# A decoder layer with experts on Trainium2: one block to the end, the feed-forward part reordered, bias and residual on TensorE

## The chip, the core and the metric

The program runs on one NeuronCore of one Trainium2 chip. The metric is the device time in microseconds (us). The engines are TensorE (PE in the profile, its weight loads PEld), VectorE (DVE), ScalarE (ACT), GpSimd (POOL) and SyncE (SP, which here only issues DMAs). Each engine works through a queue of its own in program order; engines wait for one another at semaphores. TensorE's clock has two levels, 1.2 and 2.4 GHz; the profile gives the granted clock as a share of full speed.

## The reference

16 sequences of 128 tokens and 128 features pass through a convolution mixer, a self-attention and a cross-attention of 16 heads, a feed-forward layer of 512 and, last, a small layer per token: the first 16 tokens of a sequence have an expert each, the other 112 share one. After every part stands a norm. Cut to what follows the attentions:

```python
h = gelu(x @ fc1_w + fc1_b)
x = layernorm(x + h @ fc2_w + fc2_b, ln3_g, ln3_b)
...
x = _layernorm(x + xattn)                       # x4 in the kernel
xe = x[:, :16];  y = _layernorm(xe, g_e, b_e)
out_e = gelu(einsum('bnd,ndh->bnh', y, W1_e) + b1_e) @ W2_e + b2_e      # an expert per token
xr = x[:, 16:];  out_s = gelu(_layernorm(xr, g_s, b_s) @ W1_s + b1_s) @ W2_s + b2_s
out = _layernorm(x + concatenate([out_e, out_s], axis=1))
```

## The kernel before

Every engine's queue is written out by hand in Python, as calls of small helpers. `mixer_and_attentions` is one block: the mixer works on pairs of sequences, the attentions on 32 items (16 sequences, twice), in a software pipeline over `p`. In a step TensorE runs the projections of item p + 1, the transposes of item p - 1 (`transposes`, four quarters), the output projection of item p - 2 (`out_proj`, L485), scores and `p_v` (L469). After the loop (L593 to L602) it does the first feed-forward layer (`hidden`, L236) of groups 0 and 1, mixed with the last items, and the second layer (`fc2_sum`, L253) of group 0. A group is four sequences, a chunk 128 of the 512 hidden features; `hidden` multiplies a chunk in three fp32r passes (a product of high and low parts) into banks 0 to 3. ScalarE applies the gelu (`gelu_hidden`, L244) from the bank to `hT`, of which there are two.

`feed_forward` (L1163) is a second block: no engine enters it before all have left the first. For each of the four groups VectorE computes `residual3` (the sum and its moments), `gained` and `outer_sums` (ln3 and the sum of the outer residual, with its moments), `outer_shift`, `experts_inputs`, `output_sum`, `output_statistics`, `output_shift`. The powers to -0.5 are POOL's (`inverse_ln3`, `inverse_outer` for the inner and the outer norm in one instruction, `inverse_out`), and POOL adds the second bias to X4 (`second_bias`, L1550, 128x512). ScalarE applies the norms (`z_normal`, `outer_normal`, `z_affine`, `output`) and the gelus. TensorE transposes (`z_transposes`, L1247), runs the shared first layer (`shared_w1`, L1256), the shared second layer (`shared_w2`, L1261) and, at the end, the 16 experts: `experts_w1` (L1269) needs the transposed tokens of all groups, `experts_w2` their gelu; VectorE's `experts_sums` adds the tokens' own rows (`xE`), which went through DRAM, and `experts_output` normalises. The queue of VectorE in that block (L1491 to L1525) sets the order in which groups overlap. SP loads both expert weights at the start of the block (L1219), parks X4's expert rows, reads them back, and stores four groups and four quarters of experts.

## Time and profile before

| | us |
|---|---|
| median of 3 runs | 522.64 (522.31 to 524.3) |
| the profiled execution's own time | 525.09 |
| its span, first to last instruction | 522.5 |
| TensorE busy | 473.1 |
| VectorE busy | 387.5 |
| ScalarE busy | 367.9 |
| POOL busy | 257.0 |
| mean granted clock of TensorE | 0.968 |

The span is the part of an execution between its first and its last instruction. Busy times of engines overlap, so they don't add up to it. A row of a timeline has the start, the duration, the engine, the line, the operation, the tile written and the tiles read, the shapes, how many alike were merged, and in brackets how long the engine was idle before it and what ended that.

### The profile page before, as it was taken

To read this page: it belongs to the slowest core of one execution; us is meant where nothing else is said; L and a number is where in the kernel's file an instruction comes from. 1 tells how busy PE (TensorE), PEld (TensorE's weight loads), DVE (VectorE), ACT (ScalarE), POOL (GpSimd) and SP (SyncE) were. 2 spreads that over 40 slices of the span, in tenths; PEclk is the share of its full clock that TensorE was granted. 3 is DMA by queue.
4 is the path that set the end of the run, shared out by engine and by line. 5 is a ranking of instruction groups with operands and counts; after the bars stand their busy time and mean duration, and the time that the engine had idled before them with its cause. 6 is when DMAs were issued, how large, how long until landed. Compare 5 with 4: busy or idle time off the path is not lost. (4 is left out here: it accounts for less than half of the span.)

```text
span 522.5 us, 14070 instructions
## 1 busy us (share of the span) xinstructions
PE 473.1 (91%) x4624; PEld 435.1 (83%) x4624; DVE 387.5 (74%) x1848; ACT 367.9 (70%) x1393; POOL 257.0 (49%) x343
## 2 busy tenths in 40 slices
PE   4789889999998989999999999999999998987573
PEld 4678779989998989999999999999999977876462
DVE  4667678888888887877887788778778776379832
ACT  3547877868686878887777777777778767537551
POOL 1443356666566565554445454455544455344530
PEclk9899899999999999999999999999999999999955
DMA  8830000000000004000000000000000000040003
GB/s 241 261 138 2 0 4 1 2 2 2 1 3 1 2 2 120 3 2 1 3 1 3 3 2 2 2 1 3 1 3 3 2 2 2 0 162 4 6 13 80
DMA packets 15719, 14.17 MB, mean 27 GB/s; under 512 B 2848, under 2 KB 13344, under 8 KB 15520
## 3 DMA queue, kind: packets, MB, share of 16 engines
q1 hardware_dynamic: 14240, 12.88, 7.9%
q8 instruction: 37, 0.61, 0.5%
q10 hardware_dynamic: 1408, 0.40, 0.4%
q14 instruction: 34, 0.28, 0.2%
HBM read 12.10 MB, written 1.18 MB: 25 GB/s over the span
## 5 line engine op out<-in xcount | busy, mean ns | idle before, releaser
L611 ACT ACTIVATE P<-P,at_negmax 128x128 f32<-128x128 f32 x512 | 198.9, 396 | 83.3 <-DVE at_negmax L788 83.3
L1038 POOL TENSOR_TENSOR P<-P,at_inv 128x512 f32<-128x512 f32 x128 | 136.4, 1076 | 129.9 <-DVE at_inv L798 129.8
L814 DVE COPY at_PT<-late_bank 128x512 f32<-128x512 f32 x128 | 87.7, 688 | 36.7 <-PE late_bank L448 36.5
L788 DVE CUSTOM_DVE_ANT_0 P<-late_bank,maskb 128x128 f32<-128x128 f32 x512 | 111.3, 286 | 1.5 <-PE late_bank L465 1.5
L611 ACT ACTIVATION_READ_ACCUMULATOR P<-P,at_negmax 128x1 f32 x512 | 100.1, 195 | 0.0
L448 PE MATMUL late_bank<-ident,P 128*128 128x128 f32 x512 | 77.0, 274 | 4.6 <-DVE at_negmax L788 2.8
L448 PEld LDWEIGHTS late_bank<-ident,P 128*128 128x128 f32 x512 | 59.9, 141 | 11.1 <-issue 6.4
L465 PE MATMUL late_bank<-at_k,at_q 64*128 64x128 f32 x1024 | 65.8, 278 | 0.9 <-DVE at_k L806 0.9
L465 PEld LDWEIGHTS late_bank<-at_k,at_q 64*128 64x128 f32 x1024 | 59.7, 188 | 4.8 <-issue 1.2
L480 PE MATMUL late_bank<-at_PT,V 128*64 128x128 f32 x1024 | 63.0, 276 | 0.0
L480 PEld LDWEIGHTS late_bank<-at_PT,V 128*64 128x64 f32 x1024 | 55.2, 137 | 3.9
L806 DVE COPY at_k<-late_bank 128x512 f32<-128x512 f32 x64 | 44.2, 691 | 12.6 <-PE late_bank L75 11.4
L788 DVE DVE_READ_ACCUMULATOR2_ANT at_negmax<- 128x1 f32 x512 | 42.5, 83 | 0.0
L621 ACT ACTIVATE at_q<-late_bank 128x512 f32<-128x512 f32 x64 | 37.6, 587 | 4.1 <-PE late_bank L75 4.1
L1056 POOL TENSOR_TENSOR at_N<-at_N,row_ln_g 128x128 f32<-128x128 f32 x32 | 14.7, 460 | 48.8 <-DVE at_N L839 48.8
L630 ACT ACTIVATE V<-late_bank 128x512 f32<-128x512 f32 x64 | 37.5, 586 | 0.0
L496 PE MATMUL late_bank<-wo_sa,at_OT 128*128 128x128 f32 x256 | 31.6, 276 | 3.6 <-DVE x1T_lo L936 3.6
L638 ACT ACTIVATE at_OT<-late_bank 128x512 f32<-128x512 f32 x64 | 34.1, 586 | 0.0
L496 PEld LDWEIGHTS late_bank<-wo_sa,at_OT 128*128 128x128 f32 x256 | 29.8, 192 | 4.6 <-issue 4.6
L522 PE MATMUL late_bank<-xT_hi,w_hi 128*128 128x256 f32 x72 | 23.2, 323 | 9.9 <-DVE xT_lo L857 7.0
L496 PE MATMUL late_bank<-wo_ca,at_OT 128*128 128x128 f32 x256 | 31.2, 275 | 0.0
L496 PEld LDWEIGHTS late_bank<-wo_ca,at_OT 128*128 128x128 f32 x256 | 29.9, 192 | 0.1
(177 smaller groups left out, 1062.3 us busy)
## 6 DMA issues: line engine op xcount, KB each, us to landing
ctxT_raw<-in_ctxT SPq DMA_DIRECT2D x1, 1024.0 KB, 9.3
out<-xres SPq DMA_DIRECT2D x4, 224.0 KB, 2.9
x<-in_xT SPq DMA_DIRECT2D x1, 768.0 KB, 9.7
xres<-in_x SPq DMA_DIRECT2D x1, 768.0 KB, 13.1
tap_rows<-in_short_wT SPq DMA_DIRECT2D x3, 192.0 KB, 4.4
sa_wq_raw<-in_sa_wq SPq DMA_DIRECT2D x1, 512.0 KB, 7.7
sa_wk_raw<-in_sa_wk SPq DMA_DIRECT2D x1, 512.0 KB, 8.8
sa_wv_raw<-in_sa_wv SPq DMA_DIRECT2D x1, 512.0 KB, 9.8
```

What stands on the lines that cost most here:

```text
L448: last = nc.tensor.transpose(banks[T_BANK[g % 2]][:, h * 128:(h + 1) * 128], P[:, n % 2, HQ * g + h, :], k.ident[:])
L465: last = nc.tensor.matmul(score_bank(h), q[rows, t % 2, h // 2, pair], kk[rows, t % 2, h // 2, pair], start=True, stop=True)
L480: last = nc.tensor.matmul(banks[O_BANK[h // 8]][part:part + 64, h // 2 % 4 * 128:(h // 2 % 4 + 1) * 128], V[:, n % 2, h * DH:(h + 1) * DH] ...
L496: last = nc.tensor.matmul(banks[W_BANK][:, 0:128], OT[:, n % 2, c, :], out_w[att(n)][:, c, :], start=(c == 0), stop=(c == H // 2 - 1))
L611: last = nc.scalar.activation(P[:, n % 2, h, :], P[:, n % 2, h, :], ACT.Exp, scale=-1.0, bias=negmax[:, n % 2, h:h + 1], accum_out=total[: ...
L621: nc.scalar.activation(q[:, t % 2, u:u + 2, :], banks[UNIT_BANK[0]][:].rearrange("p (h l) -> p h l", h=2), ACT.Copy, scale=NEG_SCALE).then ...
L630: nc.scalar.activation(V[:, n % 2, half * 512:(half + 1) * 512], banks[V_BANK][:], ACT.Copy).then_inc(v_ok, 1)
L638: nc.scalar.activation(OT[:, n % 2, 4 * o:4 * o + 4, :], banks[O_BANK[o]][:].rearrange("p (c l) -> p c l", c=4), ACT.Copy).then_inc(ot_ok, 1)
L788: last = nc.vector.tensor_tensor_reduce(P[:, n % 2, h, :], score_bank(h), k.maskb[:, cols(n)], scale=1.0, scalar=3.0e38, op0=ALU.add, op1= ...
L806: nc.vector.tensor_copy(kk[:, t % 2, u - 1:u + 1, :], banks[UNIT_BANK[1]][:].rearrange("p (h l) -> p h l", h=2)).then_inc(k_ok, 1)
L814: nc.vector.tensor_copy(PT[:, HQ * g:HQ * g + HQ, :], banks[T_BANK[g % 2]][:].rearrange("p (h l) -> p h l", h=HQ)).then_inc(pt_ok, 1)
L1038: nc.gpsimd.tensor_tensor(tile, tile, inv[:, n % 2, HQ * g:HQ * g + HQ].unsqueeze(2).to_broadcast([128, HQ, 128]), ALU.mult).then_inc(norm ...
```

## The change

The body of `feed_forward` moves into the block of `mixer_and_attentions`; there is one block. Its tiles lie where queries and keys and where the weights of self-attention lay. Step p = 32 of the loop is written out and mixed with first-layer chunks. `hidden` uses banks 0 and 1 in turn, `hT` has three parts, and two first-layer chunks of the next group stand ahead of each second layer. The inner and outer powers on POOL become two instructions of 4 columns. POOL's `second_bias` goes; TensorE adds the bias (in high and low parts, times an identity) into the bank of the shared second layer before it, one bank per group, and for groups 2 and 3 also X4 (`add_x4`), so that their statistics and norms read the bank (`SUMMED = 2`). The experts' bias is added alike (`experts_second_bias`). Half of group 3's inner norm (`z_normal_rest`) and all of group 3's last norm (`last_output`) are VectorE's. The shared gelu covers all 128 tokens. Constants for the bias are made at p = 18 on ScalarE (`bias_high`) and VectorE (`bias_low`). The order of all queues in the feed-forward part is new; ScalarE issues two of the experts' four stores.

Three places follow, by the order of instructions. TensorE at the handover, before: item 31's last transposes, the output projection of item 30, `p_v` of item 31, the first chunk.

```order
L448 MATMUL late_bank3<-ident,P 128x128 x4
L496 MATMUL late_bank7<-wo_ca,at_OT 128x128 x8
L480 MATMUL late_bank4<-at_PT,V 64x128 x8
L480 MATMUL late_bank5<-at_PT,V 64x128 x8
L505 MATMUL late_bank7<-ident,at_X 128x128
L73 MATMUL late_bank0<-x1T_hi,fc1_hi 128x512
```

The same place now, from the second quarter of the transposes on.

```order
L534 MATMUL late_bank3<-ident,P 128x128 x4
L72 MATMUL late_bank0<-x1T_hi,fc1_hi 128x512
L73 MATMUL late_bank0<-x1T_lo,fc1_hi 128x512
L74 MATMUL late_bank0<-x1T_hi,fc1_lo 128x512
L72 MATMUL late_bank1<-x1T_hi,fc1_hi 128x512
L73 MATMUL late_bank1<-x1T_lo,fc1_hi 128x512
L74 MATMUL late_bank1<-x1T_hi,fc1_lo 128x512
L669 MATMUL late_bank6<-bias2_hi,ident_r 128x512
L669 MATMUL late_bank6<-bias2_lo,ident_r 128x512
L534 MATMUL late_bank2<-ident,P 128x128 x4
L534 MATMUL late_bank3<-ident,P 128x128 x4
L582 MATMUL late_bank7<-wo_ca,at_OT 128x128 x8
```

Two chunks of group 0 and the bias of group 0 moved between the second and the third quarter.

VectorE from group 3's residual to its outer sums, before (`ffR` is the residual, `xres` the output sum of group 1).

```order
L1395 TENSOR_TENSOR ffR<-late_bank4,xres 128x512
L1384 BN_STATS ffstats<-ffR 128x6 x4
L1388 BN_AGGR ffmv<-ffstats 128x2 x4
L1399 TENSOR_SCALAR ffvar<-ffmv 128x4
L1449 TENSOR_TENSOR xres<-late_bank7,x1 128x512
L1384 BN_STATS ffstats<-xres 128x6 x4
L1388 BN_AGGR ffmv<-ffstats 128x2 x4
L1455 TENSOR_SCALAR ffvar<-ffmv 128x4
L1407 SCALAR_TENSOR_TENSOR N3<-ffR,ffmv,ln3_g 128x128 x4
L1418 SCALAR_TENSOR_TENSOR N3<-N3,ffrstd,x1 128x128 x4
L1384 BN_STATS ffstats<-N3 128x6 x4
```

The same place now.

```order
L1262 TENSOR_TENSOR ffR<-late_bank4,xres 128x512
L1299 SCALAR_TENSOR_TENSOR ffshift<-ffmv,ffrstd 128x4
L1250 BN_STATS ffstats<-ffR 128x6 x4
L1254 BN_AGGR ffmv<-ffstats 128x2 x4
L1268 TENSOR_SCALAR ffvar<-ffmv 128x4
L1304 SCALAR_TENSOR_TENSOR ffshift<-ffmv,ffrstd 128x4
L1276 SCALAR_TENSOR_TENSOR N3<-ffR,ffmv,ln3_g 128x128 x4
L1323 TENSOR_TENSOR zE<-late_bank5,gainT 128x64
L1327 TENSOR_TENSOR zE<-zE,shiftT 128x64
L1287 SCALAR_TENSOR_TENSOR N3<-N3,ffrstd,x1 128x128 x4
L1250 BN_STATS ffstats<-N3 128x6 x4
```

The output sum and statistics of group 1 are gone from here (those of group 0 from group 2's place alike), and the shifts of group 2 came in.

TensorE's last rows, before: transposes of group 3, shared first layer, experts around the shared second layer.

```order
L1252 MATMUL late_bank5<-ident,N5 128x128 x4
L1259 MATMUL late_bank6<-zT,w1s 128x512
L1274 MATMUL late_bank0<-zE,w1e 128x16 x3
L1265 MATMUL late_bank7<-w2,gT 128x128 x4
L1274 MATMUL late_bank0<-zE,w1e 128x16 x13
L1283 MATMUL late_bank1<-w2e,hE 32x128 x16
```

TensorE's last rows now.

```order
L669 MATMUL late_bank0<-bias2_hi,ident_r 128x512
L669 MATMUL late_bank0<-bias2_lo,ident_r 128x512
L697 MATMUL late_bank4<-bias2_hi,select 128x128 x4
L697 MATMUL late_bank4<-bias2_lo,select 128x128 x4
L674 MATMUL late_bank3<-x1,ident 128x512
L648 MATMUL late_bank5<-ident,N5 128x128 x4
L679 MATMUL late_bank3<-w2,gT 128x128 x4
L689 MATMUL late_bank1<-zE,w1e 128x16 x16
L657 MATMUL late_bank7<-zT,w1s 128x512
L707 MATMUL late_bank4<-w2e,hE 32x128 x16
L674 MATMUL late_bank0<-x1,ident 128x512
L679 MATMUL late_bank0<-w2,gT 128x128 x4
```

The experts' first layer stands ahead of group 3's shared first layer, and group 3's shared second layer is the last matmul of all; five rows of bias and X4 stand ahead of the transposes.

The diff, cut to its core (the helpers that only moved are left out):

```diff
+    k.overlay(ctx, allocate_self_weights, allocate_last)
...
-    k.hT = (k.V[:].rearrange("p b (c l) -> p (b c l)", l=128).rearrange("p (c b l) -> p c b l", b=GRP, l=128),
-            k.P[:, 0].rearrange("p (c b) l -> p c b l", b=GRP))
+    k.hT = tuple(k.P[:, i].rearrange("p (c b) l -> p c b l", b=GRP) for i in range(2)) + (
+        k.V[:].rearrange("p b (c l) -> p (b c l)", l=128).rearrange("p (c b l) -> p c b l", b=GRP, l=128),)
...
-def hidden(k, pe, g, blocks=range(FF // 128)):
-
-    for c in blocks:
-        wait(pe, k.h_ok, 4 * g + c - 3)
-        mm_split(k.nc, k.late_banks[c][:], k.fc1, np.s_[:, c * 128:(c + 1) * 128], k.x1T,
+def hidden(k, pe, g, chunks=range(FF // 128)):
+
+    for c in chunks:
+        wait(pe, k.h_ok, 4 * g + c - 1)
+        mm_split(k.nc, k.late_banks[c % 2][:], k.fc1, np.s_[:, c * 128:(c + 1) * 128], k.x1T,
                  np.s_[:, g * GCOLS:(g + 1) * GCOLS]).then_inc(k.fc1_mm, 1)
 
 
-def gelu_hidden(k, act, g):
-    for c in range(FF // 128):
+def gelu_hidden(k, act, g, chunks=range(FF // 128)):
+    for c in chunks:
         act.wait_ge(k.fc1_mm, 4 * g + c + 1)
         if c == 0:
-            wait(act, k.fc2_mm, g - 1)
-        k.nc.scalar.activation(k.hT[g % 2][:, c], k.late_banks[c][:].rearrange("p (b l) -> p b l", b=GRP), ACT.Gelu,
+            wait(act, k.fc2_mm, g - 2)
+        k.nc.scalar.activation(k.hT[g % 3][:, c], k.late_banks[c % 2][:].rearrange("p (b l) -> p b l", b=GRP), ACT.Gelu,
                                bias=k.fc1_b[:, c:c + 1]).then_inc(k.h_ok, 1)
...
+            sp.wait_ge(s_mm, 2 * ITEMS)
...
+            sp.wait_ge(ne_ok, 1)
+            for i in (0, 1):
+                store_experts(sp, i)
+            store_group(sp, LAST)
...
+            def second_bias(g):
+
+                if g == 0:
+                    pe.wait_ge(k.bias_lo, 1)
+                    pe.wait_ge(v_ok, 2 * ITEMS)
+                elif g < LAST:
+                    pe.wait_ge(pt_ok, 4 * ITEMS)
+                else:
+                    pe.wait_ge(k.h_ok, 4 * NGRP - 1)
+                for part in (k.bias2.hi, k.bias2.lo):
+                    nc.tensor.matmul(quarter(W2_BANK[g]), k.ident_r[:], part[:].unsqueeze(1).to_broadcast([128, GRP, 128]),
+                                     start=(part is k.bias2.hi), stop=False)
+
+            def add_x4(g):
+                pe.wait_ge(x4_ok, g + 1)
+                nc.tensor.matmul(banks[W2_BANK[g]][:], k.ident[:], X4[:, group(g)], start=False, stop=False)
...
+            def experts_second_bias():
+                pe.wait_ge(r3_ok, NGRP)
+                for part in (k.bias2.hi, k.bias2.lo):
+                    for c in range(NEXP // EQ):
+                        nc.tensor.matmul(banks[E2_BANK][:, c * 128:(c + 1) * 128],
+                                         k.select[0:NEXP, c].rearrange("e i s -> e (i s)"), part[0:NEXP, :],
+                                         start=(part is k.bias2.hi and c == 0), stop=False)
...
+            x_transpose(ITEMS - 4)
+            transposes(ITEMS - 1, 0)
+            transposes(ITEMS - 1, 1)
+            pe.wait_ge(k.ff_lo, 1)
+            pe.wait_ge(max_ok, 4 * ITEMS)
+            wait_result(0)
+            hidden(k, pe, 0, (0, 1))
+            second_bias(0)
+            transposes(ITEMS - 1, 2)
+            transposes(ITEMS - 1, 3)
+            out_proj(ITEMS - 2)
+            p_v(ITEMS - 1)
             x_transpose(ITEMS - 3)
-            pe.wait_ge(k.ff_lo, 1)
-            pe.wait_ge(pt_ok, 4 * ITEMS)
-            hidden(k, pe, 0)
+            hidden(k, pe, 0, (2, 3))
             out_proj(ITEMS - 1)
+            wait_result(1)
+            hidden(k, pe, 1, (0, 1))
             x_transpose(ITEMS - 2)
-            hidden(k, pe, 1)
+            fc2_sum(k, pe, 0)
             x_transpose(ITEMS - 1)
-            pe.wait_ge(ot_ok, 2 * ITEMS)
-            fc2_sum(k, pe, 0)
+            hidden(k, pe, 1, (2, 3))
+            wait_result(2)
+            hidden(k, pe, 2, (0, 1))
+            next_fc2(1)
+            hidden(k, pe, 2, (2, 3))
+            wait_result(3)
+            hidden(k, pe, 3, (0, 1))
+            next_fc2(2)
+            z_transposes(0)
+            hidden(k, pe, 3, (2, 3))
+            shared_w1(0)
+            next_fc2(3)
+            z_transposes(1)
+            second_bias(1)
+            shared_w2(0)
+            shared_w1(1)
+            z_transposes(2)
+            second_bias(2)
+            shared_w2(1)
+            shared_w1(2)
+            second_bias(3)
+            experts_second_bias()
+            add_x4(2)
+            z_transposes(3)
+            shared_w2(2)
+            experts_w1()
+            shared_w1(3)
+            experts_w2()
+            add_x4(3)
+            shared_w2(3)
...
+            gelu_hidden(k, act, 0, (0, 1))
             ot_out(ITEMS - 1, 0)
             ot_out(ITEMS - 1, 1)
-            gelu_hidden(k, act, 0)
+            xT_high(ITEMS - 3)
+            gelu_hidden(k, act, 0, (2, 3))
+            gelu_hidden(k, act, 1, (0, 1))
             xT_high(ITEMS - 2)
-            gelu_hidden(k, act, 1)
             xT_high(ITEMS - 1)
+            gelu_hidden(k, act, 1, (2, 3))
+            gelu_hidden(k, act, 2)
+            z_normal(0)
+            gelu_hidden(k, act, 3, (0, 1))
+            outer_normal(0)
+            z_affine(0)
+            gelu_hidden(k, act, 3, (2, 3))
+            z_normal(1)
+            gelu_shared(0)
+            outer_normal(1)
+            z_affine(1)
+            z_normal(2)
+            gelu_shared(1)
+            z_affine(2)
+            outer_normal(2)
+            gelu_shared(2)
+            z_normal(3)
+            outer_normal(3)
+            z_affine(3)
+            output_normal(0)
+            gelu_experts()
+            gelu_shared(3)
+            output_normal(1)
+            output_normal(2)
...
+            def bias_high():
+                nc.scalar.activation(k.ident_r[:], k.ident[:], ACT.Copy).then_inc(k.bias_hi, 1)
...
+            def z_normal_rest():
+
+                vec.wait_ge(zT_mm, LAST - 1)
+                for b in range(GRP // 2, GRP):
+                    s = LAST * GRP + b
+                    last = nc.vector.tensor_scalar(N5[:, LAST % 2, b], N3[:, LAST % 2, b], mv3[:, 1, s, 0:1],
+                                                   rstd3[:, INNER_NORM, s:s + 1], ALU.subtract, ALU.mult)
+                last.then_inc(z_half_ok, 1)
...
+            def last_output():
+                vec.wait_ge(rstd_out, NGRP)
+                for b in range(GRP):
+                    s = LAST * GRP + b
+                    last = nc.vector.tensor_scalar(res[:, s], banks[W2_BANK[LAST]][:, b * 128:(b + 1) * 128],
+                                                   mv3[:, 2, s, 0:1], rstd3[:, OUT, s:s + 1], ALU.subtract, ALU.mult)
+                last.then_inc(last_ok, 1)
...
+            residual_sum(0)
+            residual_moments(0)
             xT_low(ITEMS - 1)
+            gained(0)
+            outer_sums(0)
+            inner_shift(0)
+            residual_sum(1)
+            residual_moments(1)
+            outer_shift(0)
+            gained(1)
+            outer_sums(1)
+            inner_shift(1)
+            residual_sum(2)
+            residual_moments(2)
+            outer_shift(1)
+            experts_inputs(0)
+            gained(2)
+            outer_sums(2)
+            residual_sum(3)
+            inner_shift(2)
+            residual_moments(3)
+            outer_shift(2)
+            gained(3)
+            experts_inputs(1)
+            outer_sums(3)
+            output_sum(0)
+            inner_shift(3)
+            z_normal_rest()
+            output_statistics(0)
+            outer_shift(3)
+            experts_inputs(2)
+            experts_inputs(3)
+            output_sum(1)
+            output_shift(0)
+            output_statistics(1)
+            experts_bias()
+            output_shift(1)
+            output_statistics(2)
+            experts_sums()
+            output_shift(2)
+            output_statistics(3)
+            experts_output()
+            last_output()
...
+            def inverse_outer(g):
+                pool.wait_ge(var_inner, g + 1)
+                nc.gpsimd.tensor_tensor(rstd3[:, INNER_NORM, group(g)], var3[:, INNER_NORM, group(g)],
+                                        k.half_neg[:, 0:GRP], ALU.pow).then_inc(rstd_inner, 1)
+                pool.wait_ge(var_outer, g + 1)
+                nc.gpsimd.tensor_tensor(rstd3[:, OUTER, group(g)], var3[:, OUTER, group(g)],
+                                        k.half_neg[:, 0:GRP], ALU.pow).then_inc(rstd_outer, 1)
...
-            def second_bias(g):
-                pool.wait_ge(x4_ok, g + 1)
-                nc.gpsimd.tensor_tensor(X4[:, seqs(g)], X4[:, seqs(g)],
-                                        k.bias2[:].unsqueeze(1).to_broadcast([128, GRP, 128]),
-                                        ALU.add).then_inc(x4b, 1)
...
```

## Rows read from the trace of the kernel before

**Rows 1.** The page: busy us, share of the span and instructions per engine.

```profile
PE 473.1 (91%) x4624; PEld 435.1 (83%) x4624; DVE 387.5 (74%) x1848; ACT 367.9 (70%) x1393; POOL 257.0 (49%) x343
```

**Rows 2.** Windows: stretch, length, busy us (instructions) of each engine, clock, DMA, GB/s.

```profile
15.00:20.00 5.00, 2.81 (x16) 2.60 (x15) 2.93 (x5) 2.53 (x6) 0.84 (x1) 0.79 0.44 128
...
286.00:298.00 12.00, 12.00 (x130) 11.26 (x130) 9.41 (x48) 9.36 (x41) 5.98 (x9) 1.00 0.00 1
475.00:480.00 5.00, 4.22 (x24) 3.42 (x23) 4.41 (x25) 3.74 (x8) 2.10 (x3) 1.00 0.01 2
...
490.00:495.00 5.00, 1.85 (x10) 0.97 (x8) 4.83 (x21) 3.12 (x8) 2.46 (x2) 1.00 0.04 8
495.00:500.00 5.00, 0.79 (x4) 0.72 (x4) 3.04 (x21) 3.18 (x8) 2.64 (x2) 0.58 0.00 0
```

**Rows 3.** Timeline of VectorE at step p = 16.

```profile
262.72 0.84 DVE L851 TENSOR_TENSOR fc_lo<-fc_raw,fc_hi 128x512 fp32r<-128x512 f32 x1 [0.83 <-ACT fc_hi L652]
```

**Rows 4.** Timeline of TensorE at the handover.

```profile
443.58 1.22 PE L448 MATMUL late_bank<-ident,P 128*128 128x128 f32 x8 [1.02 <-issue]
...
448.50 0.48 PE L73 MATMUL late_bank<-x1T_hi,fc_hi 128*128 128x512 f32 x1
...
451.33 1.95 PE L496 MATMUL late_bank<-wo_ca,at_OT 128*128 128x128 f32 x16
453.75 0.30 PE L505 MATMUL late_bank<-ident,at_X 128*128 128x128 f32 x1 [0.47 <-DVE at_R L826]
...
456.74 3.73 PE L258 MATMUL late_bank<-fc,V 128*128 128x128 f32 x32
```

**Rows 5.** Timeline of VectorE in the feed-forward part.

```profile
460.81 0.69 DVE L1395 TENSOR_TENSOR ffR<-late_bank,xres 128x512 f32<-128x512 f32 x1 [2.79 <-PEq L272]
...
477.24 0.69 DVE L1449 TENSOR_TENSOR xres<-late_bank,x 128x512 f32<-128x512 f32 x1 [0.38 <-PE late_bank L1265]
...
479.38 1.14 DVE L1407 SCALAR_TENSOR_TENSOR N<-ffR,ffmv,ln_g 128x128 f32<-128x128 f32 x4
...
483.45 1.06 DVE L1443 TENSOR_TENSOR zE<-zE,shiftT 128x64 f32<-128x64 f32 x1
...
486.07 0.23 DVE L1431 SCALAR_TENSOR_TENSOR ffshift<-ffmv,ffrstd 128x4 f32<-128x4 f32 x2 [1.46 <-POOL ffrstd L1541]
...
490.56 2.15 DVE L1407 SCALAR_TENSOR_TENSOR N<-ffR,ffmv,ln_g 128x128 f32<-128x128 f32 x4
...
495.32 0.16 DVE L1425 TENSOR_SCALAR ffvar<-ffmv 128x4 f32<-128x4 f32 x1
```

**Rows 6.** Timeline of POOL: a power of 4 columns.

```profile
463.10 1.05 POOL L1535 TENSOR_TENSOR ffrstd<-ffvar,half_neg 128x4 f32<-128x4 f32 x1 [0.46 <-DVE ffvar L1399]
```

**Rows 7.** Timeline of TensorE towards the end.

```profile
486.09 1.06 PE L1265 MATMUL late_bank<-w,gT 128*128 128x128 f32 x8
...
499.21 1.12 PE L1252 MATMUL late_bank<-ident,N 128*128 128x128 f32 x4 [6.43 <-ACT N L1315]
...
504.20 2.05 PE L1265 MATMUL late_bank<-w,gT 128*128 128x128 f32 x8
506.05 5.57 PE L1274 MATMUL late_bank<-zE,w1e 128*128 128x16 f32 x26
512.67 1.94 PE L1283 MATMUL late_bank<-w2e,hE 128*32 128x128 f32 x32 [1.06 <-ACT hE L1351]
```

**Rows 8.** Timeline of VectorE: its last operation.

```profile
518.01 1.11 DVE L1487 TENSOR_SCALAR rE<-rE,mv_e,rstd_e 128x128 f32<-128x128 f32 x4 [1.12 <-POOL rstd_e L1573]
```

**Rows 9.** DMA issues (count, size, us to landing), and SP's timeline of one.

```profile
out<-xres SPq DMA_DIRECT2D x4, 224.0 KB, 2.9
...
xE<-experts_out SPq DMA_DIRECT2D x4, 32.0 KB, 2.2
...
505.63 2.58 SPq L1229 DMA_DIRECT2D xE<-experts_out  x4
```

**Rows 10.** Timeline of TensorE in the mixer.

```profile
17.53 0.39 PE L522 MATMUL late_bank<-xT_hi,w_hi 128*128 128x256 f32 x1 [2.19 <-ACT C L668]
```

658 lines of the change are left out of this document (301 added, 357 removed).

## Prediction, made before the changed kernel ran

> **What bounds the kernel now.** I read the page first, then busy time by stage, then the timeline of one engine after another from 440 us, because the change leaves the program as it was up to there. TensorE is busy 473.1 of 522.5 us [rows 1], and in the middle of the second attention it is busy 12.00 of every 12.00 us while VectorE works 9.41 and ScalarE 9.36 [rows 2]: up to about 440 us TensorE alone sets the time. After 460 us this turns. From 490 to 495 us VectorE works 4.83 of 5 us and TensorE 1.85 [rows 2], so the feed-forward part is a chain on VectorE. After 495 us no engine is full: group 3 passes alone through transposes, experts, sums and norm, with TensorE at clock 0.50. I take three stretches: handover (441.35 to 460.81), VectorE's stretch (460.81 to 495.48, the end of the last variance of group 3), and the end (495.48 to 522.5).
>
> **What the sum is made against.** The profiled span is 522.5 us. That execution's own time was 525.09, the median of the timed runs 522.64. I predict the median, 0.1 above the span.
>
> **Before 440 us: nothing.** New there are the bias's high part and two constants (three small ScalarE copies) and its low part on VectorE at p = 18. The same kind of pair stands at p = 16 already, larger: VectorE waits 0.83 us and works 0.84 [rows 3], and TensorE shows no idle time behind it. Its cover is VectorE's 2.6 us of slack per 12 us; without it the price would be about 1 us. The expert weights' DMAs move up to the last scores (about 431 us), behind SP's loads, where nobody waits for SP. POOL's two clearings (0.5 us each) stand in front of the norm of item 30, whose input comes 3 us later.
>
> **Handover.** In the queue of before TensorE waits 1.02 us for the last transposes and 0.47 for item 30's result, then runs all eight first-layer chunks of groups 0 and 1 before the second layer of group 0 (3.73 us from 456.74) [rows 4]. A chunk takes (451.33 - 448.50) / 4 = 0.71 us [rows 4]. Now two chunks go into the 1.02 us gap, and two chunks of group 1 stand behind the second layer: -1.42 for those two and -1.49 for the gaps. Added are 0.46 for the two bias matmuls (each 512 columns in one pass, like a third of a chunk), 0.7 for new waits (a chunk needs item 28's low part, which lands 0.5 us after the transposes, and 0.2 at the output projection). The last x transpose (0.1) goes behind, and the end of the block costs 0.34 us from 460.47 to VectorE's start at 460.81 [rows 4, 5], of which an ordinary semaphore would take 0.07: -0.4 in all. Sum -2.1: the first residual starts at 458.7. Banks 0 and 1 alone now serve the first layer, so TensorE waits for each gelu (0.69 us against 0.71): 0.3 us twice, with VectorE's chain 0.7 us or more behind TensorE at every group.
>
> **VectorE's stretch.** It lasts 34.7 us. Removed ahead of group 3's sums are the output sum and statistics of groups 0 and 1, 2.14 us each (477.24 to 479.38) [rows 5]: -4.3. Removed are POOL's adds of the second bias: under them a 0.22 us operation took 1.06, four that take 1.13 took 2.15 [rows 5], a third 0.87 in place of 0.17: 0.84 + 1.02 + 0.70 = -2.6. The waits of 0.20, 0.18, 0.21, 0.38 and 1.46 us (the last for a POOL power of 8 columns behind such an add [rows 5]) go: -2.4. New: each inner shift stands directly behind its variance and waits for a power of 4 columns, 1.05 us [rows 6] and the two semaphores: 1.2 us for groups 0 and 1, 0.5 for group 2, where the next residual stands between: +2.9. One more low part, and split shifts: +0.4. Sum -6.0: 28.7 us, to 487.4. TensorE's second layers would end 0.7, 1.5 and 1.7 us before VectorE wants them, so TensorE does not set this stretch.
>
> **A rule against a row.** A power on POOL ran from 463.10 for 1.05 us [rows 6] while VectorE multiplied with two inputs from SBUF at its usual 1.13 us, so only the 128x512 adds block. The Trainium skill, SBUF — State Buffer, section "Who interferes with whom", says that any GpSimd instruction that reads SBUF excludes a VectorE one with two SBUF inputs. By the rule VectorE's half of the last inner norm could lose up to 0.8 us under group 3's second power; by the row it loses nothing, and that is what I take.
>
> **The end.** From 487.4: output sum 0.7, shift when the power has landed (488.5), half of the inner norm on VectorE (0.5 for two, as four of the same form take 1.11 [rows 8]), statistics of group 0 (1.4), expert inputs of group 2, transposes of group 3 (0.6), expert inputs: 492.0. The outputs of groups 1 and 2 then run under the experts' matmuls. The first expert layer took 5.57 us for 13 experts at half clock [rows 7], 0.43 each, 6.9 for 16. No row has it at full clock; the shared second layer took 1.06 at full and 2.05 at half [rows 7], so 3.6, both kept for the range. At full clock: 495.7, bias and gelu 496.6, TensorE's shared first layer in between to 496.8, second expert layer (1.94 at half clock [rows 7]) 498.0, sum and statistics 2.2 to 500.2, statistics of group 3 straight from PSUM 1.5, power 1.1, last norm on VectorE 1.1 (the same form from SBUF took 1.11 for four [rows 8]; from PSUM no row, bounds 0.9 to 1.4): 504.0. The last store now is the 224 KB one, 2.9 us to landing [rows 9], and 0.4 to the end: 507.3. At half clock from the last transposes on, every TensorE piece doubles, and the shared second layer of group 2, the identity matmul on X4 and the shared layers, which stand around the experts, come onto the path: +8.4, 515.7. At half clock only from the end of the first expert layer: +3.4, 510.7.
>
> **Which clock.** The chip fell after a 2.19 us idle with little before it (0.79 over that stretch [rows 2, 10]) and before 500 us after 6.43 us [rows 2, 7]; it kept 1.00 from 490 to 495 with TensorE 1.85 of 5 us busy. In the new order TensorE has one idle of about 2.6 us (expert inputs of group 1 come late) and one of 1.5 us before the last transposes, filled up with bias matmuls. I take full clock up to somewhere in the first expert layer, the middle of 507.3 and 510.7: 509.0. The end takes 21.6 us against 27.0: -5.4. **Sum:** 522.5 - 2.1 - 6.0 - 5.4 = 509.0, the median 509.1.
>
> **Rivals.**
> 1. *Half clock before the last transposes:* 515.7. For it speak the 2.6 us idle and the two early falls; against it the run of work right behind.
> 2. *Full clock to the end:* 507.3. Against it speaks the fall after 2.19 us of idle. The Trainium skill, TensorE: Matmul & The Clock Gate, section "Part 1: The HAM clock gate", has the clock halved only after an idle stretch of the engine; by that rule this rival is the outcome, and the trace's fall at 2.19 us inside busy time doesn't fit it.
> 3. *The experts' transfer decides:* the sum of experts waits for the X4 rows parked in DRAM and read back. Before, the four issues started 1.6 us after the last X4 (at 505.63, for 2.58 us) and each landed 2.2 us after its issue [rows 9]: 5.8 us in all. Group 3's X4 is ready at 492.3, so the rows come at 498.1 against 498.0. Each microsecond more goes on the end: 510 to 511.
> 4. *Slower:* TensorE falls to half clock near 468, in the second layer of group 2, because it waits for gelus with two banks where it had four. The 13 us of TensorE work up to the shared layers of group 1 double, less 1.5 us of slack: 527. It is slower than before if the fall comes before about 472. Against it: 4.22 of 5 us busy was enough for 1.00 from 475 to 480 [rows 2], and the waits here are 0.3 us.
>
> **How the numbers follow.** Forecast 0.49, rival 1 0.22, rival 2 0.18, rival 3 0.06, rival 4 0.03, and 0.02 for something near no change. What can be told from no change is 0.5%, 2.6 us. Only the last two cases are not faster by that: faster 0.95, same 0.02, slower 0.03. The range reaches from rival 2 less 1.8 (handover and VectorE's waits smaller) to rival 1 plus 0.8: 505.5 to 516.5.
>
> **What would show it.** First residual on VectorE at 458 to 459; the last variance of group 3 near 487, with no output work before it and waits of about 1.2 us for POOL; no VectorE operation stretched by POOL; clock 1.00 past 490 us; the last norm near 505. It is wrong if TensorE's second layers make VectorE wait, if a power blocks VectorE, or if the clock is 0.50 before 488 us.

## The result

| | before | changed |
|---|---|---|
| median of 5 runs, us | 524.3 (522.31 to 525.47) | 507.18 (506.07 to 509.53) |
| ratio to before | 1 | 0.9678, 95% interval 0.9656 to 0.970 |
| profiled execution: own time, span | 525.09, 522.5 | 509.53, 507.7 |
| mean granted clock in it | 0.968 | 0.988 |

The forecast was 509.1 us in 505.5 to 516.5. The time before had been 522.64 us as the median of three runs. The changed kernel's other four executions have spans of 504.3 to 505.5 us; the profiled one is the slowest of the five. So the medians differ by 17.1 us and the two profiled spans by 14.8. That matters below.

The three stretches of the prediction, each read in the profiled execution as there (first x transpose of item 28, first residual on VectorE, end of the last inner variance of group 3, end of the span):

| us | before | predicted | changed |
|---|---|---|---|
| start of the handover | 441.35 | 441.35 | 440.70 |
| handover | 19.46 | 17.4 | 16.15 |
| VectorE's stretch | 34.67 | 28.7 | 28.04 |
| the end | 27.02 | 21.6 | 22.81 |
| span | 522.5 | 509.0 | 507.7 |

The differences are -0.65, -3.31, -6.63 and -4.21, together -14.8 us.

### The profile after

The page's line of busy times, which answers to [rows 1]:

```profile
PE 471.4 (93%) x4644; PEld 432.8 (85%) x4644; DVE 384.4 (76%) x1852; ACT 368.0 (72%) x1390; POOL 252.4 (50%) x342
```

Busy time hardly changed, by 1.7 us on TensorE and 3.1 on VectorE. The 14.8 us are waits, and pieces that no longer stand in the chain.

Windows of the changed kernel (columns as in [rows 2]), the first in the mixer:

```profile
50.00:60.00 10.00, 7.41 (x70) 6.40 (x69) 8.66 (x44) 8.49 (x37) 5.59 (x6) 1.00 0.00 0
440.00:455.00 15.00, 15.00 (x136) 13.58 (x132) 6.07 (x19) 8.10 (x14) 6.25 (x13) 1.00 0.01 2
480.00:485.00 5.00, 2.91 (x17) 2.34 (x18) 4.79 (x28) 3.85 (x10) 1.33 (x3) 1.00 0.00 0
485.00:490.00 5.00, 4.01 (x20) 2.82 (x19) 3.29 (x19) 3.20 (x8) 2.89 (x3) 0.84 0.04 7
490.00:495.00 5.00, 5.00 (x39) 5.00 (x38) 2.14 (x12) 2.32 (x5) 1.01 (x1) 0.81 0.13 34
495.00:500.00 5.00, 5.00 (x42) 2.65 (x42) 3.21 (x16) 2.65 (x6) 1.01 (x1) 0.66 0.23 56
```

The first one bears on the 0.65 us: the clock was 1.00 here in this execution and 0.83 before, in a part that the change doesn't touch. Just before that clock fell, at 55.5 us, the changed kernel lay 0.56 us behind (the same matmul on `sa_wq` at 54.48 us against 53.92), and at the first x transpose of the attentions (97.08 us against 97.82) 0.74 ahead. From there to the handover it is 343.5 us before and 343.6 now, so what is new at p = 18 costs nothing that shows. The second says that TensorE never waits in the handover now. The last three show the clock at half in parts of 485 to 500 us, where before it was at half from 495.8 us to the end.

The handover on TensorE, the answer to [rows 4]:

```profile
440.70 0.33 PE L591 MATMUL late_bank<-ident,at_X 128*128 128x128 f32 x1
440.86 1.04 PE L534 MATMUL late_bank<-ident,P 128*128 128x128 f32 x8
441.65 0.48 PE L72 MATMUL late_bank<-x1T_hi,fc_hi 128*128 128x512 f32 x1
...
443.58 1.03 PE L534 MATMUL late_bank<-ident,P 128*128 128x128 f32 x8
...
453.08 3.74 PE L289 MATMUL late_bank<-fc,P 128*128 128x128 f32 x32
```

The two chunks and the bias stand between the halves of the transposes, and no row has an idle time in brackets. The first chunk follows the transposes at once: the low part it needs was there.

VectorE's stretch, the answer to [rows 5] (first residual, the first wait for a power, a multiplication that ran under a POOL power, the last inner variance):

```profile
456.85 0.69 DVE L1262 TENSOR_TENSOR ffR<-late_bank,xres 128x512 f32<-128x512 f32 x1 [2.25 <-PE late_bank L289]
...
464.13 0.17 DVE L1299 SCALAR_TENSOR_TENSOR ffshift<-ffmv,ffrstd 128x4 f32<-128x4 f32 x1 [1.05 <-POOL ffrstd L1601]
...
480.72 1.14 DVE L1276 SCALAR_TENSOR_TENSOR N<-ffR,ffmv,ln_g 128x128 f32<-128x128 f32 x4
...
484.73 0.16 DVE L1294 TENSOR_SCALAR ffvar<-ffmv 128x4 f32<-128x4 f32 x1
```

All waits in it, from the view of waits of that stretch (us in total, times, the longest):

```profile
DVE ffshift L1299 <- POOL ffrstd L1601: 2.6, 3, 1.1
...
DVE N L1287 <- POOL ffrstd L1596: 0.2, 1, 0.2
```

Four waits, 2.74 us in all, where before five made 2.43. Every one is for a POOL power.

The end on TensorE and the last norm on VectorE, which answer to [rows 7] and [rows 8]:

```profile
488.47 1.08 PE L648 MATMUL late_bank<-ident,N 128*128 128x128 f32 x4 [0.98 <-DVE zE L1323]
489.35 1.91 PE L679 MATMUL late_bank<-w,gT 128*128 128x128 f32 x8
491.06 4.03 PE L689 MATMUL late_bank<-zE,w1e 128*128 128x16 f32 x32
494.93 1.74 PE L657 MATMUL late_bank<-zT,w1s 128*128 128x512 f32 x2
496.60 1.94 PE L707 MATMUL late_bank<-w2e,hE 128*32 128x128 f32 x32
498.47 1.22 PE L674 MATMUL late_bank<-x,ident 128*128 128x512 f32 x2
```
```profile
503.45 1.37 DVE L1355 TENSOR_SCALAR xres<-late_bank,ffmv,ffrstd 128x128 f32<-128x128 f32 x4
```

Read with durations in hand: the second layer took 1.06 us at full clock before [rows 7] and 1.91 here, so half; then the first expert layer runs at full clock for most of its length, and the shared first layer and the second expert layer (1.94, as at half clock in [rows 7]) are at half again. TensorE is busy without a gap from 488.47 on, and the clock rises and falls inside that.

### The profile page after: what moved, and what is told of

Same layout as the page of the kernel before. It is cut to its first block, busy times and chain, and to the rows that moved or that the text cites. A ratio compares the mean times of both kernels' runs of the same rounds, so it can differ in the third digit from the quotient of the medians.

```text
span 507.7 us, 14097 instructions
## 1 busy us (share of the span) xinstructions
PE 471.4 (93%) x4644; PEld 432.8 (85%) x4644; DVE 384.4 (76%) x1852; ACT 368.0 (72%) x1390; POOL 252.4 (50%) x342
## 4 chain that ended last, share of the span: by engine, by line
PE 77%; DVE 12%; issue 3%; POOL 2%; ACT 2%; DMA 2%; SPq 1%; POOLq 0%; DVEq 0%; ACTq 0%
PE late_bank L582 11%; PE late_bank L566 11%; PE late_bank L551 11%; PE late_bank L534 11%; PE late_bank L72 9%; PE late_bank L74 9%; PE late_bank L73 9%; DMA x<-in_xT 2%; DVE ffstats L1250 2%; PE late_bank L591 1%; DVE P L1078 1%; ACT P L817 1%; DVE N L1287 1%; PE late_bank L608 1%; DVE at_PT L1104 1%
## 5 line engine op out<-in xcount | busy, mean ns | idle before, releaser
L817 ACT ACTIVATION_READ_ACCUMULATOR P<-P,at_negmax 128x1 f32 x512 | 101.9, 199 | 0.0
```

The lines of the kernel that those rows point to most:

```text
L817: last = nc.scalar.activation(P[:, n % 2, h, :], P[:, n % 2, h, :], ACT.Exp, scale=-1.0, bias=negmax[:, n % 2, h:h + 1], accum_out=total[: ...
```

## The experiments

Start, handover, stretch and end are read as above, in each kernel's profiled execution; the four add up to its span. "Half" is where after 480 us TensorE's pieces take their half-clock durations.

| kernel | median us | ratio to before (95%) | start of the handover | handover | stretch | end | half clock, about |
|---|---|---|---|---|---|---|---|
| changed kernel | 507.18 | 0.9678 (0.9656 to 0.970) | 440.70 | 16.15 | 28.04 | 22.81 | 488.4 to 491.8, 495.2 to 498.6 |
| e1 before, no POOL add | 523.89 | 0.9988 (0.9964 to 1.0011) | 438.92 | 19.47 | 33.64 | 27.07 | from 490 on |
| e2 POOL adds | 513.08 | 0.977 (0.9721 to 0.982) | 439.30 | 16.16 | 31.90 | 22.44 | 484 to 487.5 |
| e3 POOL powers | 506.89 | 0.9655 (0.9624 to 0.9686) | 440.08 | 16.15 | 28.02 | 20.35 | 481.4 to 485 |
| e4 sums early | 512.21 | 0.9762 (0.9728 to 0.9796) | 441.24 | 16.16 | 30.15 | 23.85 | 484.7 to 489, again after 496 |
| e5 chunks first | 509.80 | 0.9698 (0.9652 to 0.9744) | 442.88 | 17.82 | 28.03 | 20.07 | 485.9 to 488.5 |
| e6 fill | 507.85 | 0.9664 (0.9612 to 0.9715) | 442.76 | 16.16 | 28.03 | 21.45 | 495.4 to 499 |
| e7 norms on ScalarE | 507.73 | 0.9663 (0.9621 to 0.9704) | 441.52 | 16.16 | 28.03 | 21.29 | 482.9 to 486 |
| e8 sums on VectorE | 509.26 | 0.9687 (0.9642 to 0.9732) | 442.36 | 16.16 | 28.03 | 21.85 | 485 to 488.3, 495 to 498.5 |
| e9 changed kernel again | 509.72 | 0.970 (0.9662 to 0.9738) | 440.99 | 16.14 | 28.03 | 20.24 | 482.4 to 485.7 |
| e10 reordered end | 506.71 | 0.9639 (0.9609 to 0.9669) | 441.29 | 16.15 | 26.91 | 20.45 | none before 499 |
| e11 the same and fill | 506.70 | 0.9647 (0.9614 to 0.9681) | 439.16 | 16.16 | 26.91 | 20.37 | none before 497 |
| e12 late shift | 507.19 | 0.9663 (0.964 to 0.9687) | 439.92 | 16.16 | 26.91 | 23.11 | 491.2 to about 498 |

Handover and stretch repeat to 0.02 us from kernel to kernel where their order is the same. The end doesn't, and neither does the time before the handover, which none of these edits touches: it starts between 438.92 and 442.88 us. All of that scatter arises ahead of the first x transpose of the attentions, at 95.4 to 99.4 us; from there to the handover it is 343.5 to 343.7 us in every profile. For a part it goes with the clock from 50 to 65 us: 1.00 where the handover starts at 438.9 to 441.0, 0.89 at 441.2 to 441.5 and 0.77 at 442.4 to 442.9. The medians scatter with both. So I judge handover and stretch by the traces and only large effects by the medians.

### e1: the kernel before without POOL's adds

```diff
-            second_bias(0)        # and (1), (2), (3)
...
-                vec.wait_ge(x4b, g + 1)
+                vec.wait_ge(x4_ok, g + 1)
```

(SP's wait before it parks X4's rows changes in the same way)

> The kernel before without POOL's four 128x512 adds of the second bias (left out of the result). Theory: an add of this size holds VectorE up while it multiplies with two inputs from SBUF, 0.84 + 1.02 + 0.70 us in VectorE's stretch, and one power waited behind such an add. VectorE's stretch goes from 34.7 to about 31.7 us, its operations there show their usual 1.13, 0.22 and 0.17 us, and the time falls by 2.6 to 3.4 us. Rival, the long operations have another cause and POOL's adds cost nothing: the stretch stays within 0.5 us and so does the time.

Measured: the time is the same (0.9988, interval 0.9964 to 1.0011, which a gain of 1 us would fit too), the stretch 1.03 us shorter. VectorE's timeline at the places of [rows 5], and one earlier:

```profile
471.69 0.22 DVE L1439 TENSOR_TENSOR zE<-late_bank,gainT 128x64 f32<-128x64 f32 x1 [0.88 <-ACT zT L1330]
...
481.02 0.23 DVE L1443 TENSOR_TENSOR zE<-zE,shiftT 128x64 f32<-128x64 f32 x1
...
482.61 0.23 DVE L1431 SCALAR_TENSOR_TENSOR ffshift<-ffmv,ffrstd 128x4 f32<-128x4 f32 x2 [1.29 <-POOL ffrstd L1541]
483.86 0.69 DVE L1395 TENSOR_TENSOR ffR<-late_bank,xres 128x512 f32<-128x512 f32 x1 [1.02 <-PE late_bank L258]
...
488.13 1.14 DVE L1407 SCALAR_TENSOR_TENSOR N<-ffR,ffmv,ln_g 128x128 f32<-128x128 f32 x4
```

The long operations are short again, 0.23 in place of 1.06 and 1.14 in place of 2.15, so the adds were their cause. But of the 2.56 us only 1.03 arrive. The wait for ScalarE's zT grows from 0.21 to 0.88, and a wait of 1.02 us for the second layer of group 3 is new. The stretched operations had been lying over waits. In the order of before, TensorE and ScalarE were next in line.

### e2 and e3: POOL's adds and powers in the changed kernel

```diff
             inverse_ln3(0)
+            extra(0)              # behind each group's first power
             inverse_outer(0)
...
+                nc.gpsimd.tensor_tensor(k.spare[:], k.spare[:], k.ln3_g[:].unsqueeze(1).to_broadcast([128, GRP, 128]),
+                                        ALU.add).then_inc(added, 1)                      # e2
+                nc.gpsimd.tensor_tensor(k.spare[:, 0, 0:6], k.spare[:, 0, 0:6], k.half_neg[:, 0:6],
+                                        ALU.pow).then_inc(added, 1)                      # e3
```

> The changed kernel with four extra 128x512 POOL adds on a tile that nobody reads, each directly behind a group's first power, where POOL is idle for about 3 us and VectorE multiplies with two inputs from SBUF. No power starts later by it. Theory (the adds block VectorE): each adds 0.7 to 1.0 us to VectorE's stretch, 28.0 to 31 to 32 us, and 3 to 4 us to the time. Rival (POOL's work costs only where a power queues behind it): stretch 28.0, time unchanged.

> The same as the run with extra adds, but each extra instruction is a power of 6 columns, about 1.3 us long like the add. Theory (only large elementwise work blocks, a power does not, since it hardly reads): VectorE's operations keep 1.14 us, stretch 28.0, time within 0.5 us of the changed kernel. Rival (any POOL instruction on SBUF excludes a VectorE one with two SBUF inputs): the four 1.14 us operations under it take up to 2.3, stretch and time grow by about 4 us.

POOL and VectorE in e2, then in e3, at the same place of group 0:

```profile
458.75 1.30 POOL L1611 TENSOR_TENSOR spare<-spare,ln_g 128x512 f32<-128x512 f32 x1
```
```profile
458.95 2.03 DVE L1289 SCALAR_TENSOR_TENSOR N<-N,ffrstd,x 128x128 f32<-128x128 f32 x4
```
```profile
459.52 1.36 POOL L1611 TENSOR_TENSOR spare<-spare,half_neg 128x6 f32<-128x6 f32 x1
```
```profile
459.72 1.14 DVE L1289 SCALAR_TENSOR_TENSOR N<-N,ffrstd,x 128x128 f32<-128x128 f32 x4
```

Both POOL instructions last 1.3 us and lie over the same multiplication with two inputs from SBUF. Under the add it takes 2.03 us, under the power 1.14. Over the four groups the add costs 3.88 us of stretch (31.90 against 28.02), all of it on the chain; the power costs nothing. The time of e2 is 6.2 us above e3's (513.08 against 506.89), more than the 3 to 4 expected; in the two profiles the end adds 2.09 us. That settles the rule against the row: the Trainium skill, SBUF — State Buffer, section "Who interferes with whom", would have the power exclude VectorE too, and it doesn't here.

e2 also shows the transfer of the experts' rows as the limiter, VectorE's wait at the experts' sum:

```profile
500.64 0.69 DVE L1370 TENSOR_TENSOR rE<-late_bank,xE 128x512 f32<-128x512 f32 x1 [2.71 <-DMA xE<-experts_out]
```

One of the four landings took 3.9 us there where the others took 2.2 to 2.3.

### e4: one group's output work back into the stretch

```diff
             outer_shift(2)
+            output_sum(0)
+            output_statistics(0)
             gained(3)
```

(the same two calls go from behind `outer_sums(3)` and `z_normal_rest()`)

> The changed kernel with output sum and statistics of group 0 ahead of group 3's multiplications on VectorE, as before the change (those of group 1 can't go there, its second layer is not done). My sum booked 2.14 us a group for having them out of VectorE's stretch. Expected: last variance of group 3 later by 2.1 us. Behind it the two pieces stood in the wait for the inner power (0.68 us, cost 0.2) and ahead of group 2's expert inputs (1.4 us), so the last transposes come about 1.0 us later and the time grows by 1.0 us (0.7 to 1.4). If VectorE's own chain alone decides, it grows by 2.1; if the end waits for something else, by nothing.

The stretch grew by 2.12 us, the booked price of a group. The time grew by about 5 us against 507.2, more than any case of mine. Its profiled span is 3.7 us above the first one of the changed kernel: 0.5 from before the handover, 2.1 from the stretch, 1.0 from the end. TensorE's timeline shows where the end grew:

```profile
484.75 1.09 PE L648 MATMUL late_bank<-ident,N 128*128 128x128 f32 x4 [4.58 <-issue]
...
486.49 1.91 PE L679 MATMUL late_bank<-w,gT 128*128 128x128 f32 x8
...
492.27 0.60 PE L648 MATMUL late_bank<-ident,N 128*128 128x128 f32 x4
```

TensorE now waits 4.58 us for group 2's transposes, not 2.47, and comes out of it at half clock. The bias, the second layer of group 1 and the identity matmuls, which had 1 us of slack, then end behind VectorE, and the last transposes start 4.72 us behind the end of the stretch; in the changed kernel it was 3.58, in e9 4.00. A second fall lies in the experts' part.

### e5: the handover's chunks back in front

```diff
-            fc2_sum(k, pe, 0)
-            x_transpose(ITEMS - 1)
             hidden(k, pe, 1, (2, 3))
+            fc2_sum(k, pe, 0)
+            x_transpose(ITEMS - 1)
```

(ScalarE's two gelus move in the same way)

> The changed kernel with group 1's last two first-layer chunks ahead of group 0's second layer again, as before the change. My sum booked 1.42 us for having them behind it. Theory: from the x transpose of item 28 to the first residual 16.15 + 1.4 = 17.6 us, and all of it reaches the end: time +1.4 us. Rival: TensorE is full from 455 to 475 us in the changed kernel (4.8 to 5.0 of every 5 us), so it must do these chunks anyway and the second group's second layer only ends when it did: the first residual is 1.4 us later, but the second residual not, and the time grows by 0 to 0.4 us.

Handover 17.82, +1.66 us. The second residual starts 7.36 us behind the first, as in the changed kernel, so nothing of it is regained: the rival falls, though TensorE is full there. Its chunks are early enough for VectorE wherever they stand behind the first second layer. The median is 2.6 us higher, more than these 1.4 to 1.7; in the profile the handover starts 2.2 us later, and the end is 2.7 us shorter.

### e6: TensorE's idle time filled

```diff
+            fill(9)               # 9 matmuls of 512 columns into bank 1, overwritten later
             z_transposes(2)
...
+            fill(3)
             z_transposes(3)
```

> The changed kernel with 12 extra matmuls of 512 columns into a bank that is overwritten later: 9 in TensorE's idle of 2.5 us ahead of the transposes of group 2, 3 ahead of those of group 3. Theory (the clock falls because of this idle, and the half-clock pieces lie on the path): the granted clock is 1.00 from 480 us to the end of the first expert layer, the stretch behind VectorE's last inner variance goes from 22.8 us to 20.4, and the time falls by 1 to 2.5 us against the changed kernel, with less spread. Rival (the experts' matmuls of 16 columns, or chance, decide the clock): still 0.8 or less in part of 485 to 500 us and the time within 0.7 us.

```profile
491.93 3.64 PE L689 MATMUL late_bank<-zE,w1e 128*128 128x16 f32 x32
495.42 2.00 PE L657 MATMUL late_bank<-zT,w1s 128*128 128x512 f32 x2
497.35 1.81 PE L707 MATMUL late_bank<-w2e,hE 128*32 128x128 f32 x32
```

The clock stayed at 1.00 up to 495 us, as expected, and then fell behind the experts' narrow matmuls. End 21.45, time 507.85: no gain. A fall was avoided that had cost little, and the one that costs came all the same. That is one profile; e9 shows how far such a place can move by chance, so it doesn't tell whether the filling has a part in the second fall.

### e7 and e8: the last norms and the residual sums back

```diff
-            z_normal_rest()
-            last_output()
+            output_shift(3)       # ahead of experts_output(); ScalarE runs output_normal(3)
```

> The changed kernel with all of group 3's inner norm and the last norm on ScalarE, as before the change. Theory: the inner norm's second half costs nothing either way, since the last transposes wait for VectorE's expert inputs of group 2 (ready 488.5) and ScalarE would be done at 487.8; the last norm comes 0.4 us later (a shift on VectorE of 0.16, a semaphore, 1.50 on ScalarE against 1.37). Time +0.4 us. Rival (both halves are on the path): +0.8 for the inner norm and 0.4 for the last, +1.2 us.

The last transposes start 4.05 us behind the stretch (489.76 against 485.71) with the inner norm on ScalarE, and 4.00 to 4.06 with it on two engines (e9, e3), so VectorE's half is worth nothing there. But in all three TensorE had come through half clock and started them without a wait, right behind its own matmul on X4, while ScalarE's norm in e7 ended at 489.62 us, 0.14 before them. What the half is worth when TensorE is in time, as in the first profile (3.58 us), isn't shown. From the end of group 3's last variance to the end of the span it is 6.30 us, against 5.43 in e3: the last norm on VectorE is worth 0.9 us, not 0.4. The shift for ScalarE stands ahead of the experts' norm and waits for the power, so the experts' rows and their two stores are late too, and the last store queues behind them on SP.

For e8 `SUMMED` is 4, `add_x4(2)` and `add_x4(3)` go, `output_sum(2)` and `(3)` are VectorE's:

> The changed kernel with the residual sums of groups 2 and 3 on VectorE, as before the change, in place of the identity matmuls. Theory: the sum of group 2 (0.69 us) falls into VectorE's wait for the experts, the one of group 3 lies on the path: +0.7 us. Rival: without the identity matmuls (1 us of TensorE work, 512 columns wide, ahead of the last transposes) TensorE idles 2 us there and the clock is at half through the experts: +2.5 to 4 us.

From the experts' sum to the end it is 9.59 us (498.81 to 508.4), against 9.12 in e3: the identity matmul of group 3 is worth 0.5 us, the sum of 0.69 less what the last norm gains from SBUF, 1.11 against 1.37. The clock was at half twice, as in the changed kernel that has the matmuls, so the rival has nothing for it.

### e9: the changed kernel once more

> The changed kernel once more, unchanged. The two earlier stretches are the same to 0.05 us in every run of the changed order (16.16 and 28.03 us), so those are expected again. The end took 22.8 us in its first profile and 20.1 to 21.9 in its variants, by where the clock stood at half. Theory: this is chance of each execution, not the kernel: the end here lies between 20.1 and 22.8 us, with the half-clock pieces at another place than in the first profile, and the median again within 1 us of 507.2. Rival: the kernel itself fixes where the clock falls: half at 488.4 to 491.8 and from 495.2 again, end 22.8.

```profile
482.36 1.09 PE L648 MATMUL late_bank<-ident,N 128*128 128x128 f32 x4 [2.46 <-issue]
...
489.16 0.60 PE L648 MATMUL late_bank<-ident,N 128*128 128x128 f32 x4
489.59 1.06 PE L679 MATMUL late_bank<-w,gT 128*128 128x128 f32 x8
490.49 3.64 PE L689 MATMUL late_bank<-zE,w1e 128*128 128x16 f32 x32
493.98 1.10 PE L657 MATMUL late_bank<-zT,w1s 128*128 128x512 f32 x2
495.19 1.08 PE L707 MATMUL late_bank<-w2e,hE 128*32 128x128 f32 x32
```

The same program, the same idle of 2.46 us, but now the clock fell with its end, was back before 486.2 us, and everything from the last transposes on ran at full clock: end 20.24 us, 2.57 less than in the first profile. TensorE's pieces ahead of the last transposes have slack, those behind have none. The first profile had twice as long at half clock, so this pair alone doesn't tell length from place. e6 does: it has a single fall as e9 has, but behind the last transposes, and its end is 21.45 us. The median, 509.72, is 2.5 us above the first one; I had expected it within 1 us. Three of the six executions took 507.2 to 508.3 us and three 511.2 to 511.8. The mean granted clock was 0.991 in each of the three faster ones and 0.984, 0.979 and 0.979 in the slower ones. By 2 x (1 - clock) x span that is an estimated 9 us at half clock against 16 to 21. So the 4 us go with the clock, but no trace shows where in those executions it lay: in the mixer, where the profiles differ by up to 4 us, or in the end.

### e10 to e12: a version meant to be faster

```diff
-            experts_w1()
+            experts_w1(range(0, 5))
             shared_w1(3)
-            experts_w2()
+            experts_w1(range(5, 11))
             add_x4(3)
+            experts_w1(range(11, NEXP))
             shared_w2(3)
+            experts_w2()
...
-            inner_shift(0)
             residual_sum(1)
+            inner_shift(0)        # and residual_sum(2) ahead of inner_shift(1)
```

(ScalarE has the last norm; group 3's statistics and its store go ahead of the experts')

> A version meant to be faster. The shared first layer and the identity matmul of group 3 stand between the experts' small matmuls, so that wide matmuls come every 1 to 2 us, and group 3's shared second layer and its statistics come ahead of the experts' second layer; group 3's output norm is ScalarE's and its store goes ahead of the experts'. The next residual stands ahead of the inner shift for groups 1 and 2 also. Theory: the stretch on VectorE falls from 28.03 to 27.3 (only the wait for TensorE's second layer is left), the clock is 1.00 through the experts, the experts' sum comes 1.5 us later than at full clock before, but only 6.8 us stand behind it in place of 9.2: the time falls by 1 to 2.5 us against the changed kernel. Rival: the wide matmuls don't hold the clock, and the 1.9 us that they put ahead of the experts' second layer cost what the shorter tail gives: within 0.7 us.

> The version with the reordered end and, in addition, 9 matmuls of 512 columns in TensorE's idle ahead of group 2's transposes. In the run with these alone the clock stayed at 1.00 up to 495 us and fell in the experts' small matmuls instead. Theory (both the idle and the small matmuls let the clock fall): with the wide ones among the experts' matmuls there is no fall before the end, and it is faster than the version without them by 0.3 to 1.5 us. Rival (the fall is not tied to either): the clock falls somewhere between 480 and 500 us and the time is that of the version without them.

> The version with the reordered end, with group 3's output shift behind the experts' statistics in place of ahead of them: there VectorE waited 0.52 us for POOL's power. Theory: the experts' path alone sets the end now, so the experts' norm starts 0.5 us earlier and the time falls by 0.5 us against that version, near 506.2 us. Rival: POOL's power for group 3 or ScalarE's norm and the 224 KB store become the end: no gain, or 0.3 us more.

Moving the shift gave 1.12 us of stretch, 26.91 against 28.03. What is left there are two waits for TensorE, 0.65 and 0.52 us, and two for POOL's powers, 0.18 and 0.35:

```profile
464.33 0.69 DVE L1262 TENSOR_TENSOR ffR<-late_bank,xres 128x512 f32<-128x512 f32 x1 [0.65 <-PE late_bank L289]
```

The reordered end gave nothing: 20.45 against 20.24 us. The second expert layer ends 1.3 us later behind the stretch than in e3, and 8.0 us stand behind it, not 6.8, since the statistics of group 3 and the shift's wait of 0.52 us got into the chain. Against the changed kernel in the same comparison the median is 3 us lower (506.71 against 509.72), but the ratios' intervals overlap, and the traces show only some 1 us. The three faster executions of e9 are 0.6 to 1.3 us above e10's usual 506.6 to 506.9. Against the first 507.18 it is 0.5.

e11 is not faster than e10. In both the clock stayed full up to the last matmul. In e12, the same TensorE queue as in e10, it fell all the same (the same matmul on X4 took 1.10 us in e10):

```profile
489.93 1.41 PE L685 MATMUL late_bank<-zE,w1e 128*128 128x16 f32 x12
491.18 1.95 PE L670 MATMUL late_bank<-x,ident 128*128 128x512 f32 x2
```

So wide matmuls between the narrow ones don't hold the clock for certain. e12's shift did what it should, 3.34 us from the experts' sum to their norm against 3.90, and yet its end is 2.7 us longer, by the clock.

## Why the prediction was right, and where its terms were off

**The number.** The time is 1.9 us below the forecast, but the change is 3.6 us larger: -17.1 by the medians in one comparison, where -13.5 was forecast. Part of the small miss is luck. An execution's own time lies 1.8 us above its span in the changed kernel's profile and 2.6 above in the one before. I booked 0.1 from span to median, because the profiled execution of before happened to be slower than its median. Against the usual span of the changed kernel, 505.4 us, the forecast of 509.0 is the same 3.6 us too high.

**The signs.** No output work and no stretched operation stood in VectorE's stretch, its longer waits were 1.05 us for POOL, no second layer made VectorE wait: as said. The first residual came at 456.85 us (458 to 459 said), the last variance ended at 484.89 (near 487), the last norm started at 503.45 (near 505). The clock was said to be 1.00 past 490 us, and it fell at 488.4. Half clock before 488 us was named as a sign of being wrong, and in e9, the same program, it fell at 482.3. So the sum of the work held, and the account of the clock didn't.

**Before 440 us: right.** From the first x transpose of the attentions to the handover nothing changed (343.5 and 343.6 us). The 0.65 us arise ahead of that, with the mixer's clock.

**Handover, -2.1 predicted, -3.3 measured.** The mechanism was right and the sum mis-sized. The step that failed is the 0.7 us of new waits: none shows. The term of two chunks, 1.42, measured 1.66 in e5. The rest, booked at -0.7, came to -1.65; without the 0.7 it would have been -1.4.

**VectorE's stretch, -6.0 predicted, -6.6 measured.** The output work was booked at 2.14 us a group and measured 2.12 in e4. The stretched operations are gone, and waits went from 2.43 to 2.74 us, where my terms made +0.5. What is left over is -0.1 in place of the +0.4 for the low part and the split shifts. One step is right only for this change as a whole: the -2.6 for the adds. Alone, in the order of before, they are worth 1.0 (e1), since TensorE's second layer and zT were nearly as late. In the new order each is worth its whole 1 us (e2). The 2.6 held, as I read e1 and e2 together, because the change also moved TensorE ahead; no run puts the adds back at their old places in the new order.

**A power doesn't block: right,** by e3 in all four groups.

**The end, -5.4 predicted, -4.2 and -6.8 measured.** My full-clock end of 19.9 us measured 20.1 to 20.4 in e3, e5 and e9. The first expert layer was estimated at 3.6 us and took 3.64. The last norm from PSUM, 1.1 taken, took 1.37. That step was sound. What I took for one outcome, the fall in the first expert layer, is one of several: in the first profile the clock was at half twice, in e9 once and where it costs nothing. The forecast of 21.6 lies between the two by its own construction as a middle, not because the chip did that.

**Rivals.** Rival 1 named the place of most falls: before the last transposes (e2 to e5, e7, e8, e9). But its price was wrong. I let half clock last to the end, and in e9 it was over at 485.7 us, while TensorE still had slack. None of the eleven executions of the changed kernel reached its 515.7 us; the slowest took 511.78. Rival 2 is what e3, e5 and e9 show behind the last transposes. Rival 3 had 0.06 and deserved more: at full clock the transfer and the second expert layer end together, with VectorE waiting 0.32 us for the rows in e7 and 2.71 in e2. Rival 4 didn't happen: from 75 to 480 us the clock was 1.00 in every profile of the new order.

**The clock rule.** The Trainium skill, TensorE: Matmul & The Clock Gate, section "Part 1: The HAM clock gate", ties half clock to idleness. The falls in or right behind idles of 2.44 to 4.58 us (e2 to e5, e7 to e9) go that way, and with the idle filled the clock stayed at 1.00 there (e6). In the first profile it stayed at 1.00 behind 2.47 us of idle and fell in the next one, of 0.98 us. e11 says nothing of the filling, since in e10 and e12 the clock stayed there too, behind 1.33 us left empty. The falls at 491 to 496 us don't go that way: in the 5 us before them TensorE was busy for 4.7 to 5.0. The Trainium skill, in the same section, also calls the warm-up at a kernel's start run-variable; here the two profiles of the same program differ in the tail.

**What stays open:** what makes the clock fall or hold, in the mixer and in the experts' part, from one execution to the next, and in which of the two the 4 us between the groups of executions in e9 arise.

## What to carry to other kernels

Time that an engine loses to a blocked port counts only as far as no other wait lies under it: take the cause away on its own, as e1 did, before booking the sum. Where two engines are nearly level, ask which of them is moved forward by the same change. And where TensorE works in short pieces at the end of a kernel, sort them by slack, and expect its time there to come out differently from run to run by 2 to 3 us. Read each stretch of the trace by itself, the untouched ones too: here a part that no edit touched moved by 4 us from profile to profile, as much as most of the effects under test.

## What the runs showed of the hardware

A POOL add of 128x512 in SBUF, 1.3 us long, adds 0.9 to 1.0 us to a VectorE operation with two inputs from SBUF under it. A POOL power of 6 columns and the same length adds nothing. The powers themselves go by their columns: 0.55 us for one, 1.01 for 4, 1.36 for 6 and 1.64 for 8, so two powers of 4 cost 0.4 more than one of 8, but the first is there 0.6 earlier. And 16-column matmuls with a weight load each took 3.64 us for 16 experts at full clock.
